# One attention stage, its value columns made quad by quad instead of batch by batch

## What is computed

```python
xh = layernorm(x).reshape(B, S, H, dh)            # B=2, S=1024, H=16 heads, dh=16
theta_q = xh / (1 + abs(w_q)) + b_q + t * phi_q   # the same for k
Q = concat(cos(theta_q), sin(theta_q)); K = ...   # by table lookup
theta_v = xh / (1 + abs(w_v)) + b_v
V = cos(theta_v) + sin(theta_v)
attn = softmax(causal(Q @ K.T / sqrt(2 * dh)))
out = attn @ V
theta_out = out / (1 + abs(w_out)) + b_out
x = x + cos(theta_out) + sin(theta_out)
```

## Time and profile before

| | us |
|---|---|
| median of 3 runs (1046.23 to 1047.78) | 1046.27 |
| the profiled execution | 1045.22 |
| its span | 1043.5 |
| PE busy | 913.1 (88%) |
| DVE busy | 754.9 (72%) |
| ACT busy | 601.3 (58%) |
| POOL busy | 350.1 (34%) |

### The profile page before, as it was taken

How to read it: one execution, slowest core, us unless ns; L and a number is a source line. 1 busy time by engine, 2 the same in 40 slices (tenths; PEclk the granted TensorE clock), 3 DMA queues, 4 the chain that set the end, 5 groups by cost and what they waited for, 6 DMA issues and landing times. The chain is left out here.

```text
span 1043.5 us, 20376 instructions
## 1 busy us (share of the span) xinstructions
PE 913.1 (88%) x8028; PEld 565.3 (54%) x8028; DVE 754.9 (72%) x1412; ACT 601.3 (58%) x1052; POOL 350.1 (34%) x310
## 2 busy tenths in 40 slices
PE   2778878899589799999689999998799988999996
PEld 1323333333247545565456777776699974455554
DVE  8957978895778899887768899886678865344412
ACT  4778969999567553552145555554688853332410
POOL 1314764563237231000246667675243210000000
PEclk9969989999779999999999999999899999999999
DMA  5000000000221030000130000000200000000001
GB/s 145 0 2 1 1 2 1 1 1 1 67 96 42 1 133 1 1 2 1 46 120 2 2 1 2 3 2 1 72 2 1 3 1 1 1 13 9 21 1 41
DMA packets 17502, 21.96 MB, mean 21 GB/s; under 512 B 4656, under 2 KB 14590, under 8 KB 17024
## 3 DMA queue, kind: packets, MB, share of 16 engines
q1 hardware_dynamic: 15296, 18.57, 5.5%
q10 hardware_dynamic: 2112, 2.10, 0.6%
HBM read 18.56 MB, written 2.10 MB: 20 GB/s over the span
## 5 line engine op out<-in xcount | busy, mean ns | idle before, releaser
L625 PE MATMUL t_sc<-t_qk 32*128 32x512 f32 (+3 forms) x768 | 117.2, 571 | 41.4 <-ACT t_pT L515 16.2
L515 ACT ACTIVATE t_pT<-t_sc 128x1536 f32<-128x1536 f32 x96 | 136.7, 1453 | 23.8 <-PE t_sc L625 22.9
L3081 DVE SCALAR_TENSOR_TENSOR f_h<-f_psh,f_h 128x512 f16<-128x512 f32 x64 | 43.9, 691 | 100.8 <-ACT f_h L3107 100.7
L3137 PE MATMUL f_psh<-f_h,fs_w 128*128 128x512 f16 x512 | 114.4, 379 | 1.5 <-DVE f_h L3081 1.5
L229 POOL TENSOR_SCALAR_AFFINE_SELECT t_pT<-t_pT 128x512 f32<-128x512 f32 x64 | 75.1, 1196 | 112.7 <-ACT t_pT L515 112.4
L625 PEld LDWEIGHTS t_sc<-t_qk 32*128 32x128 f32 x768 | 53.2, 203 | 104.9 <-ACT t_pT L515 61.3
L3107 ACT ACTIVATE f_h<-f_psh 128x512 f16<-128x512 f32 x64 | 38.2, 597 | 108.4 <-PE f_psh L3137 108.4
L2600 POOL TENSOR_SCALAR_AFFINE_SELECT r_att<-r_att 128x1024 f16<-128x1024 f16 x64 | 69.6, 1110 | 66.2 <-DVE r_att L2640 66.0
L645 PE MATMUL t_ot<-t_pT,t_v 128*17 128x512 f32 (+3 forms) x768 | 73.6, 511 | 9.4 <-issue 8.8
L3137 PEld LDWEIGHTS f_psh<-f_h,fs_w 128*128 128x128 f16 x512 | 49.8, 98 | 59.0 <-issue 2.0
L1896 PE MATMUL c_pso<-ck_VO,c_pT 128*128 128x256 f16 x480 | 55.0, 273 | 1.4 <-DVE c_pT L1747 1.4
(11 more groups left out here) (504 smaller groups left out, 2175.2 us busy)
## 6 DMA issues: line engine op xcount, KB each, us to landing
x<-in_x ACTq DMA_DIRECT2D x4, 512.0 KB, 7.6
out_x<-x SPq DMA_DIRECT2D x4, 512.0 KB, 2.9
r_rcos<-in_ret_cos SPq DMA_DIRECT2D x1, 1280.0 KB, 8.0
r_rsin<-in_ret_sin SPq DMA_DIRECT2D x1, 1280.0 KB, 10.5
gw_raw<-in_gateT SPq DMA_DIRECT2D x1, 1024.0 KB, 7.1
gw_raw<-in_upT SPq DMA_DIRECT2D x1, 1024.0 KB, 9.1
gw_raw<-in_downT SPq DMA_DIRECT2D x1, 1024.0 KB, 4.7
fs_k<-in_L_ffn_k SPq DMA_DIRECT2D x1, 1024.0 KB, 7.4
```

The source lines that it names most:

```text
L515: a.activation(pT[:, at:at + 3, :].rearrange("p a s -> p (a s)"), sc[n % 2][:], ACT.Exp, scale=CURVE * CURVE / math.sqrt(2 * DH)).then_inc ...
L625: last = t.matmul(sc[n % 2][:, 512 * k + at:512 * k + at + w], qk[r, g % 2, 1, P * i:P * i + P], qk[r, g % 2, 0, q0:q0 + w], start=(part = ...
L3081: v.scalar_tensor_tensor(dst[:, 1], psh[:, i % BANKS, :], 0.0, dst[:, 0], ALU.max, ALU.subtract).then_inc(lo_done, 1)
L3137: last = mm(psh[:, i % BANKS, :], l, r, start=(k == 0), stop=(k == len(todo) - 1))
```

## The change

Each quad now has its own small table lookup for the 64 value columns it needs (128x512), in buffers `va` and `vf` (quad 2's in the second half of `ou` and `of`). `pre_v(q)` and `post_v(q)` run on VectorE in the loop before the quad, the sine on ACT together with the other sines of that quad, and the square on POOL (`bend_v`). The eight instructions that normalise batch 1 go from ACT to the end of VectorE's loop 1. At the start, ACT no longer squares the second half of quad 0's `frac`; POOL does it. The gains for the values (`row_gains`) are made for 64 columns first and for 192 later. In quad 1 PE weighs slots 0 to 5 in one go after exp step 8, as in quad 0, rather than in two parts, and ACT's sines come after exp step 7.

```diff
+        def values_at(q):
+            return (ou[:, 1, :], of[:, 1, :]) if q == 2 else (va[:], vf[:])
...
             inverse_root(0)
+            bend(frac[:, 0, :]....[:, :, 512:1024], qk_pre, 2, qk_late)
+            bend_v(0)
             inverse_root(1)
             for q in range(QUADS):
+                if q == 1:
+                    bend_v(1)
...
-                if q == 3:
-                    bend(waves_of_v(1)[1], v_pre, 2, v_late)
+                if 0 < q < QUADS - 1:
+                    bend_v(q + 1)
...
             post_qk(0, 1)
-            angle_v(0)
             pre_v(0)
             variances(1)
             angles(1)
-            offsets(1)
             whole_turns(angle[:, 1, :], tmp[:])
+            fraction(angle[:, 1, :], frac[:, 1, :], tmp[:]).then_inc(qk_pre, 1)
             post_v(0)
-            fraction(angle[:, 1, :], frac[:, 1, :], tmp[:]).then_inc(qk_pre, 1)
             post_qk(1)
+            row_gains(0, 0, 1, slice(64, D))
+            pre_v(1)
...
-                if g == 2:
-                    pre_v(1)
+                if g + 1 < QUADS:
+                    pre_v(g + 1)
+                if g == 1:
+                    post_v(1)
                 front_o(g - 1, 1)
                 pre_o(g - 1)
-                if g == 1:
-                    angle_v(1)
                 if g + 1 < QUADS:
                     post_qk(g + 1)
-                if g == 3:
-                    post_v(1)
+                    post_v(g + 1)
+                if g == 1:
+                    normalise(TB, 2 * TB, xn_next)
...
                     if g == 0 and e == 7:
-                        waves(v_pre, 1, v_waves, waves_of_v(0)[0])
-                        bend(v_pre, 1, v_bent, waves_of_v(0)[1])
-                        a.wait_ge(v_ready, 1)
-                        normalise(TB, 2 * TB)
+                        waves(v_pre, 1, v_waves, values_at(0)[0])
                         waves(qk_pre, 3, qk_waves, angle[:, 1, :])
                         bend(qk_pre, 3, qk_bent, frac[:, 1, :])
+                    if g == 1 and e == 7:
+                        waves(v_pre, 2, v_waves, values_at(1)[0])
+                        waves(qk_pre, 4, qk_waves, angle[:, 0, :])
+                        waves(v_pre, 3, v_waves, values_at(2)[0])
...
-                    if g == 0 and e == 8:
+                    if g < 2 and e == 8:
                         for s in range(6):
-                            weigh(s)
-                    if g and e == 6:
+                            weigh(SLOTS * g + s)
+                    if g >= 2 and e == 6:
                         weigh(SLOTS * g)
```

More of the change, by code:

```diff
@@ L132, in table_attention @@
         sm = sb("sm", [P, 6, NT])
-        params = sb("params", [6, D])
-        twice = sb("twice", [6, H0, 2, DH])
+        va, vf = sb("va", [P, 512]), sb("vf", [P, 512])
+        params = pT[0:6, 0, 0:D]
+        twice = pT[0:6, 1, :].rearrange("p (h c d) -> p h c d", h=H0, c=2)
         cols = sb("cols", [P, 4, 6])
@@ L286, in offsets, with normalise @@
                 v.scalar_tensor_tensor(sm[:, 0, tiles], sm[:, 2, tiles], -1.0, sm[:, 4, tiles], ALU.mult, ALU.mult).then_inc(nm_ready, 1)
[L288 to L289 removed]
+            def normalise(t0, t1, done):
+                for t in range(t0, t1):
                     v.tensor_scalar(xn[:, t], both(x[:, t, :]), sm[:, 2, t:t + 1], sm[:, 4, t:t + 1],
[L291 removed]
+                                    ALU.subtract, ALU.mult).then_inc(done, 1)
             def gains(dst, w):
@@ L328, in post_qk @@
                 v.wait_ge(qk_waves, n)
-                if g < 2:
-                    v.wait_ge(qk_bent, n)
+                if g == 0 and h == 1:
+                    v.wait_ge(qk_late, 1)
+                elif g < 2:
+                    v.wait_ge(qk_bent, g + 1)
                 else:
-                    v.wait_ge(qk_late, g - 1)
+                    v.wait_ge(qk_late, g)
                 if g >= 2:
@@ L351, in pre_v @@
[L351 to L366, removed]
+            def pre_v(q):
+                b, c = q // 4, slice(64 * (q % 4), 64 * (q % 4) + 64)
+                a, f = values_at(q)
+                by_head = lambda row: row[:, c].rearrange("p (h d) -> p h d", d=DH).unsqueeze(2).broadcast_to((P, 4, TB, DH))
+                a4 = a.rearrange("p (h t d) -> p h t d", h=4, d=DH)
+                rows_ = xn[:, TB * b:TB * b + TB, 4 * (q % 4):4 * (q % 4) + 4, 0, :].rearrange("p t h d -> p h t d")
+                if q == 0:
+                    v.wait_ge(xn_ready, 4)
+                    v.wait_ge(xn_late, 4)
+                if q == 4:
+                    v.wait_ge(xn_next, TB)
+                L(v.tensor_tensor(a4, rows_, by_head(rrow[:, 0, :]), ALU.mult))
+                L(v.tensor_tensor(a4, a4, by_head(rows[:, 1, :]), ALU.add))
+                whole_turns(a, tmp[:, 0:512])
+                fraction(a, f, tmp[:, 0:512]).then_inc(v_pre, 1)
@@ new lines, in post_v @@
+            def post_v(q):
+                b, heads = q // 4, slice(4 * (q % 4), 4 * (q % 4) + 4)
+                v.wait_ge(v_waves, q + 1)
+                v.wait_ge(v_bent, q + 1)
+                cut = lambda z: z.rearrange("p (n d) -> p n d", d=DH)
+                a, f = values_at(q)
+                v.scalar_tensor_tensor(v1[:, b, heads].rearrange("p h t d -> p (h t) d")[:, :, 0:DH], cut(f), CURVE_OFF,
+                                       cut(a), ALU.add, ALU.mult).then_inc(v_ready, 1)
@@ L414, in _ @@
             v.wait_ge(s_par, 16 * 6)
-            v.tensor_copy(twice[:], both(params[:])).then_inc(par_twice, 1)
+            v.tensor_copy(twice, both(params)).then_inc(par_twice, 1)
             sums(1, 0, 0, 3)
             offsets(0)
-            normalise()
+            normalise(0, 4, xn_ready)
             v.wait_ge(par_turned, 1)
@@ L428, in _, with row_gains @@
             sums(1, 1, 4, TB)
[L430 to L433, removed]
+            def row_gains(k, w, b, c):
+                gains(rrow[:, k, c], rows[:, w, c])
+                own.mark(v.tensor_scalar(rrow[:, k, c], rrow[:, k, c], PER_RADIAN, None, ALU.mult))
+                L(v.tensor_scalar(rows[:, b, c], rows[:, b, c], PER_RADIAN, TABLE / 8.0, ALU.mult, ALU.add))
             pre_qk(0, 0)
-            pre_qk(0, 1)
+            angles(0, 1)
+            second = [piece(w, 1) for w in (angle[:, 0, :], frac[:, 0, :], tmp[:])]
+            whole_turns(second[0], second[2])
             post_qk(0, 0)
+            fraction(*second).then_inc(qk_pre, 1)
             v.wait_ge(s_row, 16 * 4)
-            row_gains(0, 0, 1)
+            row_gains(0, 0, 1, slice(0, 64))
             post_qk(0, 1)
-            angle_v(0)
             pre_v(0)
@@ L553, in _ @@
             turn_step(1)
-            for h in range(2):
-                waves(qk_pre, h + 1, qk_waves, halves(angle[:, 0, :])[:, :, 512 * h:512 * h + 512])
-                bend(qk_pre, h + 1, qk_bent, halves(frac[:, 0, :])[:, :, 512 * h:512 * h + 512])
+            waves(qk_pre, 1, qk_waves, halves(angle[:, 0, :])[:, :, 0:512])
+            bend(qk_pre, 1, qk_bent, halves(frac[:, 0, :])[:, :, 0:512])
+            waves(qk_pre, 2, qk_waves, halves(angle[:, 0, :])[:, :, 512:1024])
             for g in range(QUADS):
@@ L635, in weigh @@
                     t.wait_ge(stepped, AT[("exp", exps_for(slot), None)] + 1)
-                if s == 0 and g % 4 == 0:
-                    t.wait_ge(v_ready, b + 1)
+                if s == 0:
+                    t.wait_ge(v_ready, g + 1)
                 for j, i, at, w in PIECES[s]:
@@ L675, in _ @@
                         turn_o(g - 1, 1)
-                    if g and e == 10:
+                    if g >= 2 and e == 10:
                         for s in range(1, 6):
```

36 lines of the change are left out of this document (12 added, 24 removed).

## The result

The changed kernel takes 1051.99 us, the kernel before 1048.16 us beside it on the same chips (medians of 20 runs each): ratio 1.0035, interval 1.0024 to 1.0046. It is slower by 3.7 us, where I had forecast +2.5. Against the 1048.8 forecast it is 3.2 us over; 1.9 of these are the median of the kernel before, 1046.27 in three runs and 1048.16 in twenty. A second measurement of the same kernel gave 1.0045 (5.8 us by the medians). In the profiled executions the attention stage accounts for 6.5 us: the next stage begins at 286.34 for 279.86. The program behind it takes 765.1 for 763.6.

A forecast was written before the change was run, and what follows sets the result against it. VectorE's chain was to become the bound: 191.1 us of unbroken work from 50.7, copy waits to 243.2; +1.0 behind it and +1.5 for PE's clock gave 1047.7 profiled, 1048.8 predicted, range 1044 to 1053 (1035 to 1058 overall).

The forecast's parts named there:

- The chain of VectorE as the bound: First attention, `post_qk(1)` to `post_qk(7)`: VectorE busy 95% or more, with no waits at the PSUM reads.
- The rival that ACT stays the pace: First attention: POOL's work falls into VectorE's waits, a loop needs 27.1 us; -13, about 1033 us; chance 0.26.
- Start of the chain, 50.7: End of quad 0: VectorE's product for quad 1, `post_qk(1)`, starts at 50.7, 13.9 us earlier than 64.64.
- ends the second product of quad 0 at about 30.5: VectorE in quad 0, before `pre_v(0)`: its second product ends at about 30.5, against 31.4 in the kernel before.
- The other side I had given, 52: Start of the chain: if masks, now earlier and beside VectorE, cost it 0.6 each, it starts at 52.
- Unbroken work, 191.1 us: VectorE from `post_qk(1)` to `post_qk(7)`: 172.9 us of work plus 18.2 of added collisions with POOL.
- Two copies must wait for PE some 0.7 each.: VectorE's chain: `copy_o` for quads 4 and 5 waits some 0.7 us each, moving the end from 241.8 to 243.2.
- PE's clock, +1.5: Starts of quads 3 to 7: PE waits about 2 us; half of one slow start at 1.2 GHz added, 1.5 us.
- Quads 3 to 6 at 29.5 to 31 us: Sign in the first attention: these quads take 29.5 to 31 us; the forecast is wrong if they stay at 28.
- The second part moves by more than 1 us.: Sign against the forecast: the program's second part, untouched by the change, moves by more than 1 us.
- Slow PE in every quad: Quads 3 to 7 each start at 1.2 GHz, 3.1 us longer; +7.5 on top of 2.5, 1056 us; chance 0.11.
- Whole-length locks, +19: POOL beside VectorE: each mask costs 0.6 rather than 0.3, each square 0.3 more; 1068 us; chance 0.03.

The follow-up runs named there:

- e_first: Changed kernel with POOL's square of the second half of quad 0's fraction on 16 of 1024 columns: 1049.17 us, 1.0018 to the kernel before.

## Why the prediction was nearly right

*The chain of VectorE as the bound.* Right. Removing POOL's squares or its masks gave 10 to 12 us each; ACT's sines gave none. In both the slow loop 5 went as well (29.5 and 32.1 us), and in e_first's profile a shift of 1.5 us was enough for that, so not all of the 10 to 12 is VectorE's lost time. The rival that ACT stays the pace has fallen, and with it the 13 us of gain.

*Start of the chain, 50.7.* Measured 52.52. The step that failed is "ends the second product of quad 0 at about 30.5": it ended at 32.0. I had moved the square to POOL and not asked what stands beside it there. With that collision taken away it ends at 30.55, and the chain starts at 51.05. The other side I had given, 52, was for masks; the fraction beside them took 2.60 for 2.29, the 0.3 as said.

*Unbroken work, 191.1 us.* Measured: 194.0 less 6.1 at the copies, 187.9. Lost time grew by 40.4 - 23.6 = 16.8 us, where I had +18.2; the ordinary work is 1.8 less. The sum held, its parts less so: by the trace the squares grew by 11.3 (I had 8.6) and the masks by 4.8 (I had 7). A square costs 3.6, where I had 3.3; a mask 0.30, as I had. The Trainium skill, "SBUF — State Buffer", section "SBUF: two separate sides", has the loser of the port pair blocked for the whole instruction. The 3.6 for a square of 3.60 fits that better than my 3.3; the mean mask, 0.64 us alone (row 253.64 above), costs half its length. And my reason that a reciprocal isn't held up, its one input, doesn't hold: in loop 1 the reciprocal L303 kept its 1.75 us beside a square, but L308, which reads one tensor as well, took 3.71 (row 167.96 above).

```profile
74.87 1.75 DVE L303 RECIPROCAL t_rrow<-t_rrow 128x256 f32<-128x256 f32 x1
75.30 3.60 POOL L236 TENSOR_TENSOR t_frac<-t_frac 128x2048 f32<-128x2048 f32 x1
```

*"Two copies must wait for PE some 0.7 each."* This term was mis-sized: 1.4 us predicted, 6.1 measured (5.77 and about 0.3). It is the largest miss, and it is one with the next.

*PE's clock, +1.5.* I put in half of one slow start. There were three: in quad 5, inside the chain, where it comes back as the wait of 5.77; in quad 6, hidden, since the next copy waits only 0.3; and in quad 7, behind the chain, 2.13 - 0.58 = 1.55 us. Without the one in quad 5, e_first was spared 4.4 us of that wait, of which 3.4 show in the length of the loop. I had the mechanism from the earlier trace rows and took it for a matter behind the chain only.

*Sum.* Start +1.8, work -3.2, waits at copies +4.7: the chain ends at 246.5 for 243.2. The three errors add to 3.3 rather than 9.7 only because one has the other sign, which is luck. From there to the second exp step 5.6 us (5.0 predicted), +1.55 in the third. In the stage that is +6.5 for the +2.5 predicted. The runs are only 3.7 apart, so part of the 6.5 belongs to the profiled executions: that of the kernel before, 1045.22, lies 2.9 us under its median, that of the changed kernel, 1053.16, 1.2 over.

*Quads 3 to 6 at 29.5 to 31 us.* From first exp step to first exp step, quad 3 took 27.9 us, quads 4 and 6 29.3 and 30.8, and quad 5 35.1. VectorE's loops were 29.4 to 30.3 from the second on, apart from loop 5. In quads 2 and 3 the exp steps still kept ACT's 27.8, so I should have named loops and not quads. The first exp step of quad 7 came at 247.84, outside the 244 to 247 that I had given.

*"The second part moves by more than 1 us."* It moved by 1.5, and by the letter this speaks against me. But in the traces of the other kernels the same untouched part took from 762.9 to 768.2 us, so my bound was tighter than one profile can show.

*The other rivals.* Slow PE in every quad: in three of five, but at most 4.4 + 1.55 us of it were paid, where I gave that rival +7.5. Whole-length locks, +19: the price of a square is near it, that of a mask and the total aren't.

## What to carry to other kernels

Before work is moved onto an engine that looks a fifth idle, add the time it will lose beside the engine it shares a port with: here some 20 us of added work and 17 of lost time used up 20 us of waits and made the chain 16 us longer, where the removed stall had given 12. When an engine becomes the bound, take off it first whatever another engine waits for at once: 2.7 us of copies were worth 7 to 10 (PE's clock included), while 3.7 us of normalising were worth nothing, as they only moved the wait. A slow start of PE inside a loop is paid at the next thing that waits for PE, so it belongs in the chain's sum.

## What the hardware showed

- A POOL instruction can hold up even a small VectorE one: a 128x64 scale took 1.85 us beside a 1.89 us square, and 0.20 without it.
- The clock of PE after a wait isn't a matter of that wait's length alone: 2.46 us of idle before the transposes of quad 5 were followed by a granted clock of 0.50, 2.45 us in e_first by transposes at full speed. What decides it stays open.
- Many short instructions can cost nearly as much as a few long ones: in the changed kernel's chain VectorE lost 21.5 us beside six wide squares and 14.9 beside 49 masks, and either set, taken away, was followed by 10 to 12 us less program time.
- Not every VectorE instruction is held up: the reads of `ot` (128x16, L384) kept 245 to 258 ns whether POOL was at work or not, and a reciprocal of 128x256 kept its 1.75 us beside a square.
